# Cross-attention and mixture-of-experts kernel: TensorE's step reordered, output projection in full-size tiles, the norms' rstd and shift in one set, tail loop written out

## What is computed

```python
def reference(x, ctx, Wq, Wk, Wv, Wo, W1, b1, W2, b2, Wr, br, gamma, beta):
    # attention
    xn = layernorm(x)                       # over the 128 features, eps 1e-5
    q = heads(xn @ Wq.T); k = heads(ctx @ Wk.T); v = heads(ctx @ Wv.T)
    scores = where(causal, q @ k.T * 8 ** -0.5, -1e9)
    x = x + unheads(softmax(scores) @ v) @ Wo.T
    # feed-forward with experts
    z = layernorm(x)
    rw = softmax(z.mean(axis=1) @ Wr + br)  # one row of 8 per batch entry
    tk_w, tk_i = top_k(rw, 2); tk_w = softmax(tk_w)
    out = sum over the two of tk_w * (gelu(z @ W1[e] + b1[e]) @ W2[e] + b2[e])
    y = out + z
    return x + (y - mean(y)) / sqrt(var(y) + 1e-5) * gamma + beta
```

## Time and profile before

| | |
|---|---|
| median of three runs | 638.81 us (638.69 to 639.19) |
| the profiled execution | 638.1 us, span 636.3 us |
| TensorE (PE) busy | 576.2 us (91%) |
| VectorE (DVE) busy | 526.7 us (83%) |
| ScalarE (ACT) busy | 498.6 us (78%) |
| GpSimd (POOL) busy | 459.6 us (72%) |
| chain that ended last | PE 84%, ACT 5%, issue 4%, DVE 3%, POOL 2% |

### The profile page before, as it was taken

The page is one execution under the profiler, slowest core; times in us unless marked ns, Lnnn a source line. Parts: engine busy times, 40 slices in busy tenths (PEclk is TensorE's granted clock), DMA queues, the critical chain, the costliest instruction groups (busy, mean ns, idle before and its releaser), DMA issues.

```text
span 636.3 us, 19450 instructions
## 1 busy us (share of the span) xinstructions
PE 576.2 (91%) x4721; PEld 379.1 (60%) x4721; DVE 526.7 (83%) x1473; ACT 498.6 (78%) x1131; POOL 459.6 (72%) x815
## 2 busy tenths in 40 slices
PE   3899999999999999999999726999999999999762
PEld 2455555555555555555555413887888788787652
DVE  2889898898989898989898756888888888888576
ACT  3678887888787878787887626888888888888695
POOL 5688999999999999999999653756655555564233
PEclk9999999999999999999999955999999999999887
DMA  3010100001010101010020011222322331322034
GB/s 101 27 33 12 35 25 16 25 25 32 8 33 25 33 8 33 25 33 8 16 74 2 2 32 44 62 76 82 91 60 59 88 94 58 97 62 59 25 118 147
DMA packets 55583, 30.03 MB, mean 47 GB/s; under 512 B 4856, under 2 KB 54528, under 8 KB 55552
## 3 DMA queue, kind: packets, MB, share of 16 engines
q1 hardware_dynamic: 55120, 29.47, 15.9%
q10 hardware_dynamic: 432, 0.20, 0.1%
HBM read 13.00 MB, written 4.19 MB: 27 GB/s over the span
## 4 chain that ended last, share of the span: by engine, by line
PE 84%; ACT 5%; issue 4%; DVE 3%; POOL 2%; ACTq 1%; DVEq 1%; DMA 0%; POOLq 0%
PE scores_banks L350 12%; PE bank_pair L361 12%; PE bank_pair L374 7%; PE bank L387 6%; PE scores_banks L346 6%; PE scores_banks L475 5%; PE scores_banks L476 5%; PE scores_banks L477 5%; PE bank_pair L488 5%; PE bank_pair L490 5%; PE bank_pair L489 5%; PE bank L334 3%; PE bank L323 2%; ACT squares L693 2%; PE bank L327 2%
## 5 line engine op out<-in xcount | busy, mean ns | idle before, releaser
L1060 POOL TENSOR_TENSOR probs<-probs,row_sum_recip 128x512 f32<-128x512 f32 x128 | 133.6, 1044 | 19.7 <-DVE row_sum_recip L781 17.7
L582 ACT ACTIVATE probs<-scores_shifted 128x512 f32<-128x512 f32 x128 | 80.7, 631 | 52.0 <-DVE scores_shifted L775 50.7
L672 ACT ACTIVATE gelu<-scores_banks,b_expert 128x512 f32<-128x512 f32 x144 | 98.6, 691 | 27.8 <-PE scores_banks L477 21.9
L1109 POOL CAST gathered<-z_hi_lo (+1 forms) x114 | 45.5, 434 | 92.7 <-PE scores_banks L477 83.2
L765 DVE TENSOR_REDUCE row_max<-scores_banks 128x8 f32<-128x512 f32 x128 | 87.5, 683 | 24.4 <-PE scores_banks L350 24.3
L768 DVE TENSOR_REDUCE row_sum<-probs 128x8 f32<-128x512 f32 x128 | 87.1, 680 | 17.0 <-ACT probs L582 17.0
L891 DVE SCALAR_TENSOR_TENSOR zT_then_yT<-bank_pair,slot_weight,zT_then_yT x288 | 74.6, 283 | 17.3 <-issue 15.8
L591 ACT ACTIVATE probsT<-bank_pair 128x512 f32<-128x512 f32 x128 | 76.1, 595 | 14.6 <-PE bank_pair L361 13.6
L775 DVE TENSOR_TENSOR scores_shifted<-scores_banks,row_max 128x512 f32<-128x512 f32 x128 | 86.8, 678 | 0.0
L361 PE MATMUL bank_pair<-ident,probs 128*128 128x128 f32 x512 | 84.0, 286 | 2.0 <-POOL probs L1060 1.6
L350 PE MATMUL scores_banks<-k_by_head,qT 32*64 32x256 f32 x1024 | 85.5, 404 | 0.0
(11 more groups left out here) (165 smaller groups left out, 1167.3 us busy)
## 6 DMA issues: line engine op xcount, KB each, us to landing
gathered<-z_hi_lo SPq DMA_DIRECT2D x187, 64.0 KB, 1.8
x_res<-in_x SPq DMA_DIRECT2D x16, 256.0 KB, 2.7
ctxT_pair<-in_ctxT SPq DMA_DIRECT2D x32, 128.0 KB, 2.1
w_raw<-in_w SPq DMA_DIRECT2D x16, 256.0 KB, 3.1
out<-gelu SPq DMA_DIRECT2D x16, 256.0 KB, 2.2
gathered<-z_hi_lo ACTq DMA_DIRECT2D x3, 64.0 KB, 1.9
wq<-in_wq SPq DMA_DIRECT2D x1, 64.0 KB, 2.4
wk<-in_wk SPq DMA_DIRECT2D x1, 64.0 KB, 2.3
```

The costliest lines, as they stand in the source:

```text
L672: nc.scalar.activation(G[:, c, :], bank[c][:, :], ACT.Gelu, bias=b1e).then_inc(a_g if c == 0 else a_gp, 1)
L1060: nc.gpsimd.tensor_tensor(pp, pp, RC[:, k % 2, :].unsqueeze(2).to_broadcast([128, 8, S]), ALU.mult).then_inc(g_norm, 1)
```

## The change

TensorE: a step now runs scores, attend, turn, the pieces for the pair, and then the mask of the next step, which `scores` no longer contains. `project` uses all 128 columns of attnT at once (two fp32 matmuls instead of four), and ScalarE's attnT copy writes a layout that allows it. GpSimd: `rstd1` and `rstd2` are replaced by one `rstd_both` in s=2, which works on four columns (two of each norm) in one set of four instructions; the buffers are joined (MV, RS, SH) and g_sh counts sets. ScalarE's norms wait for g_sh. The tail: ScalarE's loop over o is written out, VectorE adds one x tile of four and GpSimd three.

```diff
@@ tensor
+            def mask(i, k):
+                ge(pe, v_sub, 8 * i + k - 1)
+                for rp in range(2):
+                    nc.tensor.matmul(S_ps[k % 2][:, rp, :], identb[:, :], cmask[:, :, :].rearrange("p a k -> p (a k)"),
+                                     start=True, stop=False, skip_group_check=True)
             def scores(i, k):
...
-                ge(pe, v_sub, U - 1)
-                for rp in range(2):
-                    nc.tensor.matmul(ps[:, rp, :], identb[:, :], cmask[:, :, :].rearrange("p a k -> p (a k)"),
-                                     start=True, stop=False, skip_group_check=True)
...
-                for b in range(2):
-                    for r2 in range(2):
-                        mm = nc.tensor.matmul(J1[64 * b:64 * b + 64, 0:D], AT[:, t, b, 64 * r2:64 * r2 + 64],
-                                              WOZ[:, r2, :], start=(r2 == 0), stop=(r2 == 1))
+                for r2 in range(2):
+                    mm = nc.tensor.matmul(J1[:, 0:D], AT[:, t, r2, :], WOZ[:, r2, :], start=(r2 == 0), stop=(r2 == 1))
...
+                    if not static or 0 <= U - 4 < NB:
+                        attend(i, u - 4)
                     if not static or 0 <= U - 3 < NB:
                         turn(i, u - 3)
-                    if not static or 0 <= U - 4 < NB:
-                        attend(i, u - 4)
...
+                    if not static or U + 1 < NB:
+                        mask(i, u + 1)
@@ scalar
             def norm1(P):
-                act.wait_ge(g_sh1, P + 1)
+                act.wait_ge(g_sh, P + 1)
...
             def norm2(P):
-                act.wait_ge(g_sh2, P + 1)
+                act.wait_ge(g_sh, P + 5)
...
-                        nc.scalar.activation(AT[:, t, :, :].rearrange("p b q -> p (b q)"),
-                                             A_ps[:, 0:256], ACT.Copy).then_inc(a_at, 1)
+                        nc.scalar.activation(AT[:, t, :, :].rearrange("p a (b q) -> p b a q", b=2),
+                                             A_ps[:, 0:256].rearrange("p (b a q) -> p b a q", b=2, a=2),
+                                             ACT.Copy).then_inc(a_at, 1)
...
-            with act.Fori(0, 4) as o:
+            for o in range(4):
@@ vector
-                nc.vector.tensor_tensor(YN[:, k, 0:2, :], YN[:, k, 0:2, :], X[:, bass.ds(16 * o + 4 * c, 2), :],
+                nc.vector.tensor_tensor(YN[:, k, 0:1, :], YN[:, k, 0:1, :], X[:, bass.ds(16 * o + 4 * c, 1), :],
@@ gpsimd
+            def rstd(call, par, first, second):
+                c = slice(0 if first else 2, 4 if second else 2)
+                n = c.stop - c.start
+                nc.gpsimd.tensor_tensor(RS[:, c], MV[:, par, c, 1], eps[:, 0:n], ALU.add).then_inc(g_eps, 1)
+                nc.gpsimd.tensor_scalar(SH[:, c], MV[:, par, c, 0], -1.0, None, ALU.mult).then_inc(g_eps, 1)
+                pool.wait_ge(g_eps, 2 * call + 2)
+                nc.gpsimd.tensor_tensor(RS[:, c], RS[:, c], minus_half[:, 0:n], ALU.pow).then_inc(g_rs, 1)
+                pool.wait_ge(g_rs, call + 1)
+                nc.gpsimd.tensor_tensor(SH[:, c], SH[:, c], RS[:, c], ALU.mult).then_inc(g_sh, 1)
+
+            def rstd_both(P, h, first, second):
+                if first:
+                    pool.wait_ge(v_mv1, 2 * P + 6)
+                    pool.wait_ge(a_xn, P + 2)
+                if second:
+                    pool.wait_ge(v_mv2, 2 * P - 2)
+                    ge(pool, a_z, P - 2)
+                rstd(P + 2, h, first, second)
...
-                    if s == 1 and (not static or P + 2 < NP):
-                        rstd1(P + 2)
-                    if s == 2 and (not static or 0 <= P - 2 < NP):
-                        rstd2(P - 2, h)
+                    if s == 2 and (not static or P < NP + 2):
+                        rstd_both(P, h, not static or P + 2 < NP, not static or P >= 2)
...
-                yn = YN[:, c % 4, 2:4, :]
+                yn = YN[:, c % 4, 1:4, :]
...
-                nc.gpsimd.tensor_tensor(yn, yn, X[:, bass.ds(16 * o + (4 * c + 2), 2), :], ALU.add).then_inc(g_out, 1)
+                nc.gpsimd.tensor_tensor(yn, yn, X[:, bass.ds(16 * o + (4 * c + 1), 3), :], ALU.add).then_inc(g_out, 1)
```

More of the change, by code:

```diff
@@ L433, in _ @@
             pe.wait_ge(v_setup, 4)
+            mask(0, 0)
             steps(0)
@@ L715, in stats1 @@
                 settle(dve, v_setup)
-                ge(dve, g_sh1, P)
+                ge(dve, g_sh, P - 1)
                 for k in range(2):
@@ L753, in steps @@
                     if s == 1:
-                        T, slot, k2, late = 4 * i + (2 * h - 3), (2 * h + 1) % 4, 1, not static or 0 <= P - 2 < NP
+                        T, P2, h2, k2, late = 4 * i + (2 * h - 3), P - 2, h, 1, not static or 0 <= P - 2 < NP
                     else:
-                        T, slot, k2, late = 4 * i + (2 * h - 2), (2 * h - 2) % 4, 0, not static or 0 <= P - 1 < NP
+                        T, P2, h2, k2, late = 4 * i + (2 * h - 2), P - 1, 1 - h, 0, not static or 0 <= P - 1 < NP
                     late = late and s % 2 == 1
@@ L792, in _ @@
             dve.wait_ge(d_x, 16)
-            stats1(0)
+            stats1(0, 0)
             dve.nop().then_inc(v_setup, 1)
@@ L1002, in causal_mask @@
                 pool.nop().then_inc(g_const, 1)
-            def rstd(P, mv, rs, sh, eps_sem, rs_sem, sh_sem):
-                nc.gpsimd.tensor_tensor(rs, mv[:, :, 1], eps[:, 0:2], ALU.add).then_inc(eps_sem, 1)
-                nc.gpsimd.tensor_scalar(sh, mv[:, :, 0], -1.0, None, ALU.mult).then_inc(eps_sem, 1)
-                pool.wait_ge(eps_sem, 2 * P + 2)
-                nc.gpsimd.tensor_tensor(rs, rs, minus_half[:, 0:2], ALU.pow).then_inc(rs_sem, 1)
-                pool.wait_ge(rs_sem, P + 1)
-                nc.gpsimd.tensor_tensor(sh, sh, rs, ALU.mult).then_inc(sh_sem, 1)
-            def rstd1(P):
-                pool.wait_ge(v_mv1, 2 * P + 2)
-                ge(pool, a_xn, P)
-                rstd(P, MV1[:, :, :], RS1[:, :], SH1[:, :], g_eps1, g_rs1, g_sh1)
-            def rstd2(P, h):
-                pool.wait_ge(v_mv2, 2 * P + 2)
-                ge(pool, a_z, P)
-                rstd(P, MV2[:, 2 * h:2 * h + 2, :], RS2[:, :], SH2[:, :], g_eps2, g_rs2, g_sh2)
+            def rstd(call, par, first, second):
[15 more added lines that the diff above has]
+                rstd(P + 2, h, first, second)
             def spread_k(P, par, batches):
@@ L1061, in steps @@
                                                 ALU.mult).then_inc(g_norm, 1)
-                    if s == 1 and (not static or P + 2 < NP):
-                        rstd1(P + 2)
-                    if s == 2 and (not static or 0 <= P - 2 < NP):
-                        rstd2(P - 2, h)
+                    if s == 2 and (not static or P < NP + 2):
+                        rstd_both(P, h, not static or P + 2 < NP, not static or P >= 2)
                     if s == 3 and (not static or 0 <= P - 3 < NP):
                         split_z(P - 3)
-            rstd1(0)
+            pool.wait_ge(v_mv1, 2)
+            rstd(0, 0, True, False)
             causal_mask()
@@ L1072, in _ @@
             spread_k(0, 0, range(4))
-            rstd1(1)
+            pool.wait_ge(v_mv1, 4)
+            pool.wait_ge(a_xn, 1)
+            rstd(1, 1, True, False)
             pool.wait_ge(d_late, 96)
```

38 lines of the change are left out of this document (18 added, 20 removed).

## The result

| | before | after |
|---|---|---|
| median, us | 638.79 (638.69 to 639.19) | 695.07 (694.84 to 698.58) |
| profiled execution / its span, us | 638.1 / 636.3 | 695.14 / 693.4 |
| `norm1` starts, first and last of the 30 in the steps | 23.02, 336.45 | 25.03, 401.52 |
| mean period between them, us | 10.81 | 12.98 |
| from the last `norm1` to the end of the span, us | 299.9 | 291.9 |

The ratio is 1.0888 (95% interval 1.0871 to 1.0905): slower by 56.3 us. The last `norm1` comes 65.1 us later and what stands behind it takes 8.0 us less.

The account below looks back on a forecast made before the run. TensorE was taken to bound the kernel before, the norm1 ring (12.37 us a pair) the changed one. 638.1 + 46.8 (attention) - 1.0 (drain) - 6.5 (tail) = 677.4 us, 678.1 against the median; range 662 to 692 us.

Parts of the forecast that it names:

- the ring through `norm1`: Cycle from norm1 over exp, VectorE and GpSimd's moved set back to norm1: 12.37 us a pair, chance 0.75.
- the sum: Links of the norm1 cycle added start to start: 12.11 us, with 0.26 for the wider power 12.37 us.
- The first `norm1`: First norm1 start in the loop of pairs: about 25.1 us instead of 23.02, its set standing later on GpSimd.
- third rival: TensorE's wait before attend of s=0 lowers the clock, delaying row_max of s=2: up to 717 us, chance 0.10.
- The wait lies between these: TensorE's 1.6 to 1.9 us wait placed between trace rows: busy 0.52 of 2.00 us (full clock), 0.87 of 4.00 (fallen).
- TensorE's work: TensorE's need a pair: 10.1 instead of 10.7 us, from full-size projections and fewer changes of tile form.
- The power at four columns: GpSimd's power in the joined set: 0.72 us at two columns, plus 0 to 0.52 us, middle 0.26.
- The link from the shift to `norm1`: Last link, from GpSimd's shift done to ScalarE's norm1: 0.03 us.
- `row_sum` to reciprocal: VectorE link from row_sum to the reciprocal of step s=1: 4.31 us without idle time, order unchanged.
- The tail: ScalarE's written-out loop and VectorE's shorter add: one table load left, reciprocals 1.52 us apart, -6.5 us.
- The second: Rival: norm1's shift is ready in time, so TensorE binds at 10.1 us a pair: about 611 us, chance 0.10.
- The fourth: Rival: something in the norm1 cycle is shorter, period about 11.4 us: 651 us, chance 0.05.

Follow-up runs that it names:

- norm_set_only: The kernel before with only the joined set of rstd and shift in s=2 (its buffers and waits); TensorE order, projection and tail old: 687.88 us, 1.0767.
- set_in_s1: The changed kernel with one line moved: the joined set of four columns issued in step s=1 instead of s=2: 626.91 us, 0.9807.
- set_before_norm: The changed kernel with the joined set still in s=2, but ahead of that step's normalisation: 651.86 us, 1.0201.
- filled_wait: The changed kernel with the next step's mask multiplied nine times behind the scores at s=0, while TensorE waits for attend: 680.69 us, 1.0644.
- projection_only: The kernel before with only the output projection in two full-size fp32 matmuls and the attnT copy that goes with it: 633.15 us, 0.9895.
- norms_apart: The changed kernel with the two sets of rstd and shift apart in their old places (s=1 and s=2, two columns each): 625.73 us, 0.9798.
- exp_first: The changed kernel with the joined set in s=1 and, on ScalarE at s=0, the exp ahead of the four V copies: 620.45 us, 0.9706.

## Why the prediction was right and where it was wrong

**Right: the mechanism and its size.** The loss is the ring through `norm1`, with the set behind `spread_k` and a normalisation. norm_set_only makes it alone (688 us), set_in_s1 takes it away alone, and set_before_norm takes 0.98 to 0.99 of 1.00 us off the period. The undisturbed period was 12.37 by the sum and is 12.44 and 12.60 in turn; its mean where the clock stays full is 12.50 (filled_wait). With the clock full the kernel takes 680.69 us (filled_wait), 2.6 from the forecast. The first `norm1` was put at 25.1 and is at 25.03.

**Wrong: the clock was a rival at a chance of 0.10, and neither the sum nor the range held it.** The prediction had most of the mechanism in its third rival: a wait between the two rows, and a clock that falls for some microseconds. Both are in the trace. The place where the fall reaches the ring is another: the rival names row_max of s=2 with 0.1 us to spare, and the one that waits first is row_max of s=1, 0.32 to 0.77 us in 18 of the 19 intervals; s=2 adds the smaller part (0.15 of 0.83 us in the pair shown). The step that failed is "The wait lies between these", weighed as if it were near the harmless end, and the range left out its 717 us. With the clock in it, the sum goes like this: from the first to the last `norm1`, 15.5 us more than in filled_wait, which is 0.82 us in each of 19 intervals, two pairs of three. The 1.4 us a pair of the rival was an upper end. The forecast for the profiled execution was 677.4, and it took 695.1. Of these 17.7 us the clock is 15.5; the ring, 12.50 instead of 12.37 us in 27 intervals, is 3.4; the first two intervals are -0.6, the first `norm1` -0.1 and what stands behind the last -0.5.

**A term mis-sized on the way there: TensorE's work.** The sum had 10.1 us a pair; the window 76 to 88 us holds one pair's work and has 9.91 of TensorE busy (before: 10.70 by the earlier trace rows). `turn` and what follows lost 0.08, near the 0.10 taken, but in this order the projection takes 0.44 us, not 0.55 (200.91 to 201.35):

```profile
200.41 0.66 PE L361 MATMUL bank_pair<-ident,probs 128*128 128x128 f32 x4
...
200.91 0.61 PE L386 MATMUL bank<-wo_half,attnT 128*128 128x128 f32 x4
...
201.35 0.38 PE L339 MATMUL scores_banks<-causal_mask,ident_bf 128*128 128x256 bf16 x2
...
203.10 0.61 PE L331 MATMUL bank<-wv,ctxT_pair 128*128 128x128 f32 x4
...
203.55 0.38 PE L339 MATMUL scores_banks<-causal_mask,ident_bf 128*128 128x256 bf16 x2
```

The value projection of the earlier trace rows, the nearest row, had a change of tile form ahead of it and was a poor measure: in after, behind `turn`, it takes 0.45 us (203.10 to 203.55). With attend ahead, the full-size projection does take the 0.55 of the forecast (projection_only, s=2). A faster TensorE waits longer in a ring of the same length: 2.0 to 2.3 us and not 1.6 to 1.9. That ties the clock to the rest of the change: norm_set_only, with the same ring and the slower order, waits 1.2 us and keeps the clock. Whether the order or the projection is what takes the clock was not tried. The change with its three other parts is 7.2 us slower than that one part alone, though the tail in it gains 6.

**Small terms.** The power at four columns takes 1.04 us against 0.72: +0.32, where the middle of the bounds was 0.26. The link from the shift to `norm1` was taken as 0.03 from the start of the kernel; it is 0.03 to 0.04 in the first three intervals and 0.13 to 0.15 in all later ones. `row_sum` to reciprocal was read in one pair (4.31) and is 4.20 and 4.37 in turn. The tail was right: one table load, reciprocals 1.52 us apart, and 22.56 us for the fifteen intervals (665.27 to 687.83) against 22.6. Its rows, which answer:

```profile
663.58 1.28 ACT L699 ACT_TABLE_LOAD   x1
...
668.12 0.17 DVE L940 RECIPROCAL ln_rstd<-ln_std 128x4 f32<-128x4 f32 x1
...
669.43 0.28 DVE L952 TENSOR_TENSOR gelu<-gelu,x_res 128x128 f32<-128x128 f32 x1
...
669.63 0.17 DVE L940 RECIPROCAL ln_rstd<-ln_std 128x4 f32<-128x4 f32 x1
```

The add of one tile takes 0.20 us from its start to the reciprocal, as assumed.

**The rivals.** The second (no ring, 611 us) falls: 12.44 us link by link. Its price was too good as well: with the ring out of the way (set_in_s1, norms_apart) the kernel takes 626 us, at a period of 10.7; by the timelines GpSimd's queue and a ring of exp stand in the way there, and only the second was tried (exp_first). The fourth (651 us, a shorter ring) is not what happened, but is what set_before_norm made.

## What to carry to other kernels

When a producer is moved down an in-order queue, add up the ring from its consumer back to it, not the busy time of its engine: here GpSimd was relieved of 0.9 us of work a pair and the period grew by 1.7 even where the clock stayed full. In a kernel whose engines stand within 20% of each other, removing one ring buys only the distance to the next (10.4 to 10.8 us here), so a part's gain should be priced in the kernel in which it will run. And when a ring makes TensorE wait, price the wait twice, once as time and once as clock, and let the second into the range as soon as the wait is longer than any that the trace shows harmless.

## What the runs showed of the hardware

- The granted clock fell to 0.50 behind waits of 1.9 to 2.3 us that came once in 12.4 to 13.4 us, in 19 of 29 periods; behind a wait of 1.99 us at 74.4 to 76.4 us it did not fall, nor behind one of 2.33 us up to 88.90, while it did with one of 2.33 us up to 245.50. It stayed at 1.00 in the two kernels that wait 1.2 and 1.3 us at that place (norm_set_only, set_before_norm). What decides between two such waits was not tried.
- GpSimd's power costs by width where an addition does not: 0.72 us for two columns, 1.04 for four, the additions 0.20 for both.
- The output projection as eight matmuls of half the width takes 0.60 us (before). As four full-size ones, for the same product, it takes 0.55 us behind the 32-column tiles of attend and 0.44 behind full-size work (projection_only).
